# Sorted expert stages of a four-layer gated decoder: silu products kept in PSUM, expert ranks by a scan, row loads led by four jobs, weight splits put behind the normalised rows

## The chip, the cores and the metric

One core of one Trainium2 chip. The metric is the device time of the whole kernel in microseconds, one launch, median over the runs of the same kernel. All data are float32; the large matmuls are done as three fp32r matmuls of a high and a low part of each operand.

## The reference, cut to what matters

x is 8 x 256 rows of 256. Four layers follow one another, each a gated cross attention and a gated feed-forward branch, `x = x + tanh(g) * branch(layernorm(x))`. The change touches the feed-forward branches of layers 1 and 2, both mixtures of 8 experts of which each row takes 2. Layer 2 (layer 1 has hidden size 682, no bias, no shared part, and normalises its two weights):

```python
scores = jax.nn.softmax((xt @ gate_w.T).astype(jnp.float32), axis=-1)
_, idx = jax.lax.top_k(scores + gate_bias, TOPK)
weights = jnp.take_along_axis(scores, idx, axis=1).astype(x.dtype)
y = jnp.zeros_like(xt)
for e in range(N_EXPERTS):
    gate_e = jnp.sum(jnp.where(idx == e, weights, 0.0), axis=1)
    h = jax.nn.silu(xt @ w1[e].T) * (xt @ w3[e].T)
    y = y + gate_e[:, None] * (h @ w2[e].T)
z = jax.nn.silu(xt @ sw1.T) * (xt @ sw3.T) @ sw2.T
return (y + z).reshape(shape)
```

## The kernel before

The kernel is written engine by engine; each engine has one program, in which a function per stage follows the one of the stage before, with semaphores between the engines and an order written out by hand. The two sorted expert stages are the functions `mixture` of each engine, run for `L1F` (layer 1) and `L2F` (layer 2). A stage goes like this.

**Front.** VectorE normalises the 16 tiles of 128 rows (L1230) and writes them to one SBUF tensor. TensorE transposes them (L2175), ScalarE copies them out, TensorE forms the logits (L2165), VectorE the two largest of eight per row by comparing all pairs (L1235 to L1261). TensorE then forms for each row and expert how many rows ahead of it took the same expert (L2183, L2186), and how many there are in all (L2189). VectorE adds the start of the expert's region (L1274), and the result is the row of a DRAM table where GpSimd scatters the normalised row (L772, 32 indirect DMAs). Ahead of the scatter GpSimd splits the first sets of weights (`split_set`, L759 casts to the high part, L761 subtracts for the low part): 2 sets for L1F, 5 for L2F.

**Loop.** A job is 512 rows of one expert; there are 8 fixed jobs, one an expert, and 7 whose expert and rows are read from a table of numbers computed in the front. L2F has four more ahead, the shared experts over all rows, which don't need the table. Per job: SyncE loads the rows (`rows_for`, L515), TensorE transposes them (`turned`, L2205, eight transposes), ScalarE and VectorE make the high and low part (L1318). For each tile of 128 hidden units TensorE runs 12 matmuls of 512 columns (`up`, L1736 to L1738), the half tile of L1F six; ScalarE takes silu of one bank (L1670); VectorE multiplies by the other bank (L1329), casts to the high part (L1332) and subtracts for the low one (L1333). L1F has 5 tiles and a half a job, L2F 2 (4 in a shared job). `down` forms the output of the job in two banks, ScalarE copies them out (L1457), SyncE stores them (L534). The order on TensorE is: tiles 1 to the last of job k, `turned(k + 2)`, tile 0 of job k + 1, `down(k)`. There are two row buffers, two buffers for the transposed rows, and two banks for each of the two products of a tile, so tile n + 2 uses the banks of tile n; TensorE waits for the product of n (`prod`), which frees them:

```python
if n >= 2:
    pe.wait_ge(m["prod"], at["prod"] + n - 1)
```

SyncE's program is a loop over the jobs. Step k: the row load of job k + 2; then, once `down(k)` is done, the weights of set w + ring (L487); then the two stores of the job's result. Only two sets fit in L1F, so a set is asked for when the last but one is used up; in L2F five fit.

**Back.** GpSimd gathers the two results of each row (L786, 32 indirect DMAs), VectorE adds them with their weights to x (L1358).

In what follows the loop of L1F is called A, the routed part of that of L2F is called B. Other lines named: L700 is the inverse square root on GpSimd, L1054 a copy of attention probabilities out of PSUM in other stages. `arena`, `split`, `ew`, `ewh`, `ewl`, `sil`, `lg`, `x` and `w` are SBUF tensors, `bank` is PSUM, `rows_by_expert` the DRAM table.

## Time and profile before

| | us |
|---|---|
| median of 3 runs | 3420.68 (3419.69 to 3465.46) |
| profiled execution, its own time | 3391.78 |
| its span, first to last instruction | 3390.0 |
| TensorE busy, share | 2575.8, 76% |
| VectorE busy, share | 1580.7, 47% |
| ScalarE busy, share | 872.7, 26% |
| GpSimd busy, share | 785.2, 23% |
| mean granted TensorE clock | 0.829 of full |

A granted clock of 1.0 is 2.4 GHz, of 0.5 is 1.2 GHz; a mean between is a mixture of the two. The busy shares are means over many stages, of which the change touches two. In the rows further down a bracket behind an instruction is the idle time of its engine just before it and what ended that; a wait for several semaphores is put down to the one that came last. PE is TensorE's matmuls, PEld its weight loads, DVE VectorE, ACT ScalarE, POOL GpSimd, SPq the DMAs that SyncE issues. fp32 matmuls (not fp32r) are recorded as two.

### The profile page before, as it was taken

The page shows a single profiled execution, that of the slowest core. Times are in us where ns is not written, and L with a number is a line of the kernel's source. Part 1 is how long each engine was busy: PE and PEld are TensorE (multiplying, and loading weights), DVE is VectorE, ACT ScalarE, POOL GpSimd, SP SyncE. Part 2 cuts the span into 40 slices and gives each one's busy share as a digit, 9 for nine tenths or more (in the row PEclk, how much of TensorE's full clock was granted, in tenths as well). Part 3 has the DMA queues.
Part 4 walks back from the last instruction along what each step waited for, and adds up shares of the span by engine and source line. Part 5 has one row for each costly group of instructions (what it writes and reads, how often), then busy time and mean ns, then how long its engine had stood idle before and what let it go on. Part 6 is the DMA issues. An engine that isn't in the chain of part 4 may idle for free.

```text
span 3390.0 us, 37402 instructions
## 1 busy us (share of the span) xinstructions
PE 2575.8 (76%) x13142; PEld 1918.9 (57%) x13142; DVE 1580.7 (47%) x2934; ACT 872.7 (26%) x2012; POOL 785.2 (23%) x709
## 2 busy tenths in 40 slices
PE   3795885487887728888888577673888884999998
PEld 3574554376666625555556466552555653766665
DVE  3443566256657423333334533224564554454454
ACT  1221342111111103323333112122453451232232
POOL 3103223334334133333434422213000000000000
PEclk8795676699898868888989588786896996988899
DMA  3704441122232230000000013321000000000000
GB/s 115 253 0 57 56 60 54 68 96 98 78 103 91 83 118 5 2 2 2 2 2 0 13 50 95 105 86 55 5 3 2 5 1 0 1 0 0 0 0 25
DMA packets 91147, 151.93 MB, mean 45 GB/s; under 512 B 7612, under 2 KB 75900, under 8 KB 88428
## 3 DMA queue, kind: packets, MB, share of 16 engines
q1 hardware_dynamic: 61820, 101.93, 11.1%
q0 software_dynamic: 8736, 27.76, 2.6%
q10 hardware_dynamic: 20496, 20.97, 1.7%
q8 instruction: 59, 0.97, 0.1%
q14 instruction: 36, 0.29, 0.0%
HBM read 90.51 MB, written 47.19 MB: 41 GB/s over the span
## 4 chain that ended last, share of the span: by engine, by line
PE 57%; issue 20%; DVE 10%; POOL 5%; DMA 3%; ACT 3%; SPq 1%; another core or an unknown queue 1%; ACTq 0%; DVEq 0%; POOLq 0%
PE bank L1898 11%; PE bank L1853 7%; PE bank L1736 6%; PE bank L1915 6%; PE bank L1737 5%; PE bank L1738 5%; PE bank L1939 4%; PE bank L1873 2%; DMA arena<-rows_by_expert 2%; POOL arena L786 2%; DVE nmax L1044 1%; PE bank L1987 1%; DVE split L1332 1%; PE bank L2091 1%; ACT arena L1457 1%
## 5 line engine op out<-in xcount | busy, mean ns | idle before, releaser
L1898 PE MATMUL bank<-arena 64*128 64x256 f32 x1536 | 472.4, 442 | 6.2 <-ACT arena L1457 6.2
L1898 PEld LDWEIGHTS bank<-arena 64*128 64x128 f32 x1536 | 283.0, 207 | 141.6 <-issue 108.5
L1542 ACT ACTIVATE arena<-bank,nmax 128x256 f32<-128x256 f32 x512 | 226.3, 470 | 459.8 <-DVE nmax L1044 457.8
L1915 PE MATMUL bank<-ident,arena 128*128 128x128 f32 x1536 | 272.0, 306 | 74.7 <-POOL arena L829 44.2
L1044 DVE TENSOR_REDUCE nmax<-bank 128x2 f32<-128x512 f32 x256 | 175.8, 690 | 321.0 <-PE bank L1898 316.9
L1457 ACT ACTIVATE arena<-bank 128x512 f32<-128x512 f32 (+1 forms) x346 | 198.2, 580 | 463.1 <-PE bank L1853 112.0
L1736 PE MATMUL bank<-split,ewl 128*128 128x512 f32 x514 | 227.3, 442 | 98.8 <-DVE arena L1329 86.2
L1915 PEld LDWEIGHTS bank<-ident,arena 128*128 128x128 f32 x1536 | 177.6, 151 | 210.1 <-issue 112.2
L700 POOL TENSOR_TENSOR rstd<-rstd,mhalf 128x2 f32<-128x2 f32 x40 | 28.0, 700 | 996.8 <-DVE rstd L972 839.2
L1329 DVE TENSOR_TENSOR arena<-sil,bank 128x512 f32<-128x512 f32 x136 | 93.2, 685 | 315.9 <-ACT sil L1670 300.3
L1737 PE MATMUL bank<-split,ewh 128*128 128x512 f32 x514 | 217.2, 423 | 0.0
L1738 PE MATMUL bank<-split,ewh 128*128 128x512 f32 x514 | 215.5, 419 | 0.0
L1333 DVE TENSOR_TENSOR split<-arena,split 128x512 fp32r<-128x512 f32 x136 | 211.9, 1558 | 4.7
L759 POOL CAST ewh<-ew 128x1536 fp32r<-128x1536 f32 (+1 forms) x47 | 91.6, 1948 | 500.0 <-DMA ew<-in_we 500.0
L761 POOL TENSOR_TENSOR ewl<-ew,ewh 128x1536 fp32r<-128x1536 f32 (+1 forms) x47 | 204.2, 4344 | 3.8
L1054 DVE COPY arena<-bank 128x512 f32<-128x512 f32 (+1 forms) x264 | 177.1, 674 | 55.7 <-PE bank L1915 55.6
L1670 ACT ACTIVATE sil<-bank 128x512 f32<-128x512 f32 x136 | 81.4, 598 | 440.5 <-PE bank L1738 413.6
L1736 PEld LDWEIGHTS bank<-split,ewl 128*128 128x128 f32 x514 | 107.9, 210 | 131.5 <-DVE arena L1329 71.5
L1736 PE MATMUL bank<-ewh,split 128*128 128x256 f32 x544 | 167.8, 309 | 17.7 <-DVE split L1333 10.0
L1939 PE MATMUL bank<-arena 128*17 128x256 f32 (+1 forms) x1536 | 157.3, 423 | 24.2 <-ACT arena L1457 16.6
L825 POOL TENSOR_TENSOR esum<-esum,minus 128x2 f32<-128x2 f32 x128 | 89.8, 702 | 326.8 <-ACT arena L1542 326.7
L1737 PE MATMUL bank<-ewl,split 128*128 128x256 f32 x544 | 155.8, 286 | 0.0
(394 smaller groups left out, 4764.7 us busy)
## 6 DMA issues: line engine op xcount, KB each, us to landing
ew<-in_we SPq DMA_DIRECT2D x32, 768.0 KB, 8.0
ew<-in_we SPq DMA_DIRECT2D x15, 1408.0 KB, 6.1
rows_by_expert<-mrow ACTq DMA_DIRECT2D x1, 20480.0 KB, 58.2
arena<-rows_by_expert SPq DMA_DIRECT2D x23, 512.0 KB, 6.5
rows_by_expert<-arena SPq DMA_DIRECT2D x38, 256.0 KB, 5.4
ct<-in_ctxT SPq DMA_DIRECT2D x32, 192.0 KB, 2.4
kpack<-khl SPq DMA_DIRECT2D x48, 128.0 KB, 4.4
qpack<-qhl SPq DMA_DIRECT2D x48, 128.0 KB, 5.8
```

Source lines behind the costliest of these rows:

```text
L761: nc.gpsimd.tensor_tensor(low, whole, high, ALU.subtract).then_inc(m["ws"], 1)
L1044: V.tensor_reduce(nmax[:, h, :], src.rearrange("p (t k) -> p t k", t=T), AXX, ALU.max, negate=True).then_inc(m["mx"], 1)
L1333: tt(lo, whole, hi, ALU.subtract).then_inc(m["hid"], 1)
L1457: return A(dst, src, ACT.Copy)
L1542: ins = A(prob[h % 3][:, t * S:(t + 1) * S], src[:, t * S:(t + 1) * S], ACT.Exp, bias=nmax[:, h, t:t + 1], **kw)
L1736: mm(out_, al, bh, start=start, stop=False)
L1737: mm(out_, ah, bl, start=False, stop=False)
L1738: return mm(out_, ah, bh, start=False, stop=stop)
L1853: ins = mm(dst, w[:, c, gr * P:(gr + 1) * P], of[:, c, :], start=c == 0, stop=c == kt_ - 1 and not s.split)
L1898: ins = mm(bank[h % 3][:, t * S:(t + 1) * S], q[r0:r0 + 64, gr, t * P:(t + 1) * P], kT[r0:r0 + 64, gr, :], start=True, stop=True)
L1915: ins = tr(bank[3 + k % 2][:, c0:c0 + P], prob[k % 3][:, t * S + kt * P:t * S + (kt + 1) * P], ident[:, :])
L1939: ins = mm(bank[5 + gr // 2 % 2][r0:r0 + s.vs, gr % 2 * S:(gr % 2 + 1) * S], v[:, kt, h * s.vs:(h + 1) * s.vs], probT[h % 8][:, kt * S:(kt ...
```

## The change

Five edits.

1. The product silu x second projection is written back over the PSUM bank it reads, instead of to SBUF. The cast and the subtraction that make its high and low part read it there. The bank is therefore released at the end of the subtraction (`hid`) and not of the product (`prod`).
2. The ranks: one matmul with ones gives for each tile of rows and expert the number of rows in that tile, one with the strict triangle the number ahead within the tile. VectorE sums over the tiles by a scan along a row, restarted at each expert by a constant 0/1 tensor `within`, subtracts the tile's own count, and adds the number within the tile.
3. SyncE's step k loads the rows of job k + 4 instead of k + 2; four loads stand ahead of the loop of L1F and two, as before, ahead of that of L2F. The number of row buffers stays two, so the load of k + 4 still waits until job k + 2 is transposed.
4. GpSimd waits for all 16 normalised tiles before it starts to split weights.
5. Two memsets more among the constants at the start, for `within`.

```diff
-            r.hid = [(split[:, k * 1024:k * 1024 + 512], split[:, k * 1024 + 512:k * 1024 + 1024],
-                      arena[:, k * 1024 + 512:k * 1024 + 1024]) for k in range(s.slots)]
+            r.hid = [(split[:, k * 1024:k * 1024 + 512], split[:, k * 1024 + 512:k * 1024 + 1024])
+                     for k in range(s.slots)]
...
-                if not s.shared:
-                    rows_for(0)
-                    rows_for(1)
+                for k in range(s.first, s.first + 2 if s.shared else 4):
+                    rows_for(k)
                 for k, job in enumerate(s.jobs):
                     e = k - s.first
-                    if s.first <= k + 2 < len(s.jobs):
-                        rows_for(k + 2)
+                    if max(s.first + 2, 4) <= k + 4 < len(s.jobs):
+                        rows_for(k + 4)
...
+            nc.gpsimd.memset(within[:, :, :], 1.0).then_inc(g["consts"], 1)
+            pool.wait_ge(g["consts"], done[0] + 1)
+            nc.gpsimd.memset(within[:, :, 0:1], 0.0).then_inc(g["consts"], 1)
...
                 root({"asked": asked[s.name]}, 1, rstda[:, :], rstda[:, :], mhalf[:, 0:NT])
+                pool.wait_ge(g["xn"], entered(s.name, B) * T)
                 for w in range(s.ring):
                     split_set(w)
...
-                ch.link(tt(part[2], bank[1][:, 0:NT * NE].rearrange("p (t e) -> p t e", e=NE),
-                           ebase[:, 0:1, :].broadcast_to(full), ALU.add))
+                ch.link(V.tensor_tensor_scan(upto[:, :, :].rearrange("p e t -> p (e t)"), within[:, :, :].rearrange("p e t -> p (e t)"),
+                                             bank[1][:, 0:NT * NE], 0.0, ALU.mult, ALU.add))
+                before = scr[:, 384:384 + NT * NE].rearrange("p (e t) -> p e t", e=NE)
+                ch.link(tt(before, upto[:, :, :], bank[1][:, 0:NT * NE].rearrange("p (e t) -> p e t", e=NE), ALU.subtract))
+                ch.link(tt(before, before, bank[1][:, NT * NE:2 * NT * NE].rearrange("p (e t) -> p e t", e=NE), ALU.add))
+                ch.link(tt(part[2], before.rearrange("p e t -> p t e"), ebase[:, 0:1, :].broadcast_to(full), ALU.add))
...
-                rows_of = bank[1][:, NT * NE:NT * NE + NE]
+                rows_of = upto[:, :, NT - 1]
...
-                    hi, lo, whole = (t[rr, :] for t in r.hid[n % s.slots])
+                    hi, lo = (t[rr, :] for t in r.hid[n % s.slots])
+                    whole = bank[(2 if rr.start == 0 else 0) + n % 2][rr, :]
...
-                    tt(whole, sil[n % 2][rr, :], bank[(2 if rr.start == 0 else 0) + n % 2][rr, :], ALU.mult)\
-                        .then_inc(m["prod"], 1)
+                    tt(whole, sil[n % 2][rr, :], whole, ALU.mult).then_inc(m["prod"], 1)
...
-                mm(bank[1][:, 0:NT * NE], strict[:, :], lg[:, :, :].rearrange("p t e -> p (t e)"), start=True, stop=False)
-                for t in range(NT - 1):
-                    n = NT - 1 - t
-                    mm(bank[1][:, (t + 1) * NE:NT * NE].rearrange("p (k e) -> p k e", e=NE), ones[:, :],
-                       lg[:, t:t + 1, :].broadcast_to([P, n, NE]), start=False, stop=t == NT - 2)
-                for t in range(NT):
-                    ins = mm(bank[1][:, NT * NE:NT * NE + NE], ones[:, :], lg[:, t, :], start=t == 0, stop=t == NT - 1)
+                chosen = lg[:, :, :].rearrange("p t e -> p e t")
+                for k, w in ((0, ones), (1, strict)):
+                    ins = mm(bank[1][:, k * NT * NE:(k + 1) * NT * NE].rearrange("p (e t) -> p e t", e=NE), w[:, :], chosen,
+                             start=True, stop=True)
...
                     if n >= 2:
-                        pe.wait_ge(m["prod"], at["prod"] + n - 1)
+                        pe.wait_ge(m["hid"], at["hid"] + n - 1)
```

In SyncE's queue, at the start of the loops' row loads of L2F (the first load below is that of jobs 4 and 5, `ew` a weight set, `rows_by_expert<-arena` the stores of a job), before:

```order
L515 DMA arena<-rows_by_expert 128x4x256 x2
L487 DMA ew<-in_we 128x1536 x2
L515 DMA arena<-rows_by_expert 128x4x256
L487 DMA ew<-in_we 128x1536
L534 DMA rows_by_expert<-arena 128x2x256 x2
L515 DMA arena<-rows_by_expert 128x4x256
```

and now:

```order
L516 DMA arena<-rows_by_expert 128x4x256 x4
L488 DMA ew<-in_we 128x1536 x2
L516 DMA arena<-rows_by_expert 128x4x256
L488 DMA ew<-in_we 128x1536
L534 DMA rows_by_expert<-arena 128x2x256 x2
L516 DMA arena<-rows_by_expert 128x4x256
```

The pattern behind is the same, but four row loads instead of two stand ahead of the first weight load, so that each load between two jobs' stores is that of a job two further on.

On TensorE, the ranks of L1F (`lg` holds the chosen experts; L2205 and L2211 are the first transposes of the loop), before:

```order
L2183 MATMUL bank<-lg,strict 128x128
L2186 MATMUL bank<-lg,ones 128x120
L2186 MATMUL bank<-lg,ones 128x112
L2186 MATMUL bank<-lg,ones 128x104
...
L2186 MATMUL bank<-lg,ones 128x8
L2189 MATMUL bank<-lg,ones 128x8 x16
L2205 MATMUL bank<-ident,arena 128x128 x8
```

and now:

```order
L2194 MATMUL bank<-lg,ones 128x128
L2194 MATMUL bank<-lg,strict 128x128
L2211 MATMUL bank<-ident,arena 128x128 x8
```

32 matmuls have become two. On VectorE, behind them (`upto` is the scan's result, `scr` scratch), before:

```order
L1274 TENSOR_TENSOR scr<-bank,ebase 128x128
L1277 TENSOR_TENSOR scr<-scr,larger 128x128
```

and now:

```order
L1279 SCALAR_TENSOR_TENSOR upto<-within,bank 128x128
L1282 TENSOR_TENSOR scr<-upto,bank 128x128
L1283 TENSOR_TENSOR scr<-scr,bank 128x128
L1284 TENSOR_TENSOR scr<-scr,ebase 128x128
L1286 TENSOR_TENSOR scr<-scr,larger 128x128
```

Three steps more stand between the matmuls and the slots.

## Rows read from the trace of the kernel before

**Rows 1.** Stretches of the span: busy us per engine, granted clock, DMA share, GB/s.
```profile
...
646.00:1181.00 535.00, 435.90 (x2190) 359.24 (x2190) 325.63 (x300) 89.35 (x151) 185.43 (x55) 0.90 0.26 87
...
2047.00:2285.00 238.00, 164.25 (x812) 140.69 (x810) 71.06 (x115) 49.27 (x85) 59.08 (x24) 0.81 0.33 101
...
```

**Rows 2.** Single lines: duration ns min/median/max, first and last start us, forms.
```profile
L1329 DVE TENSOR_TENSOR arena<-sil,bank x136: 673/687/692, 661.6 to 2278.2; 128x512 f32<-128x512 f32 x121, 64x512 f32<-64x512 f32 x15
L1332 DVE CAST split<-arena x136: 424/426/2798, 662.3 to 2278.9; 128x512 fp32r<-128x512 f32 x121, 64x512 fp32r<-64x512 f32 x15
L1333 DVE TENSOR_TENSOR split<-arena,split x136: 689/693/6541, 662.8 to 2279.4; 128x512 fp32r<-128x512 f32 x121, 64x512 fp32r<-64x512 f32 x15
L1054 DVE COPY arena<-bank x264: 324/681/693, 1279.5 to 3372.2; 128x512 f32<-128x512 f32 x128, 128x160 f32<-128x160 f32 x4
L1670 ACT ACTIVATE sil<-bank x136: 589/599/617, 660.9 to 2277.5; 128x512 f32<-128x512 f32 x121, 64x512 f32<-64x512 f32 x15
```

**Rows 3.** Timeline of one job of A, GpSimd and VectorE: start us, us, instruction.
```profile
1051.39 2.54 POOL L759 CAST ewh<-ew 128x2816 fp32r<-128x2816 f32 x1 [21.57 <-DMA ew<-in_we]
1054.01 6.20 POOL L761 TENSOR_TENSOR ewl<-ew,ewh 128x2816 fp32r<-128x2816 f32 x1
...
1054.25 6.51 DVE L1333 TENSOR_TENSOR split<-arena,split 128x512 fp32r<-128x512 f32 x1
```

**Rows 4.** Timeline of the same job, TensorE; in brackets idle time before and releaser.
```profile
1047.16 0.39 PE L1736 MATMUL bank<-split,ewl 128*128 128x512 f32 x1
...
1049.88 0.39 PE L1736 MATMUL bank<-split,ewl 128*128 128x512 f32 x1
...
1061.41 0.80 PE L1736 MATMUL bank<-split,ewl 128*128 128x512 f32 x1 [5.93 <-DVE arena L1329]
...
1066.97 0.47 PE L1736 MATMUL bank<-split,ewl 128*128 128x512 f32 x1 [0.93 <-DVE arena L1329]
...
1070.02 0.35 PE L1736 MATMUL bank<-ewh,split 128*128 128x256 f32 x1
```

**Rows 5.** Timeline of A, ScalarE: second result half of jobs 0, 10 and 13.
```profile
686.79 0.60 ACT L1457 ACTIVATE w<-bank 128x512 f32<-128x512 f32 x1 [4.47 <-PE bank L1738]
...
1044.37 0.60 ACT L1457 ACTIVATE w<-bank 128x512 f32<-128x512 f32 x1 [4.47 <-PE bank L1738]
...
1152.85 0.60 ACT L1457 ACTIVATE w<-bank 128x512 f32<-128x512 f32 x1 [4.47 <-PE bank L1738]
```

**Rows 6.** Waits in B (us in total, times, longest), then timeline of one job.
```profile
PE bank L2205 <- DMA arena<-rows_by_expert: 70.5, 13, 6.8
...
2099.46 0.56 SPq L515 DMA_DIRECT2D arena<-rows_by_expert  x1
...
2106.29 1.97 PE L2205 MATMUL bank<-ident,arena 128*128 128x128 f32 x8 [5.50 <-DMA arena<-rows_by_expert]
...
2112.14 0.28 PE L1736 MATMUL bank<-ewh,split 128*128 128x256 f32 x1
...
2115.02 0.40 PE L1736 MATMUL bank<-split,ewl 128*128 128x512 f32 x1
```

**Rows 7.** Waits ahead of loop A, 540 to 590.
```profile
PE bank L2175 <- DVE arena L1230: 22.5, 5, 7.7
```

**Rows 8.** Timeline ahead of loop A, and the router's first step ahead of B.
```profile
543.26 30.12 DVE L1230 TENSOR_SCALAR arena<-x,mva,rstda 128x256 f32<-128x256 f32 x16 [3.08 <-POOL rstda L700]
...
579.61 0.29 DVE L1235 COPY lg<-bank 128x128 f32<-128x128 f32 x1 [6.23 <-PE bank L2165]
...
587.86 0.79 PE L2183 MATMUL bank<-lg,strict 128*128 128x128 f32 x2 [8.29 <-DVE idle L1260]
...
601.79 0.29 DVE L1274 TENSOR_TENSOR scr<-bank,ebase 128x128 f32<-128x128 f32 x1 [12.20 <-PE bank L2189]
...
1911.37 0.29 DVE L1235 COPY lg<-bank 128x128 f32<-128x128 f32 x1 [9.84 <-PE bank L2165]
```

**Rows 9.** Waits in the shared jobs, 1940 to 2000.
```profile
ACT sil L1670 <- remote: 26.9, 2, 14.2
```

More of the change, by code:

```diff
@@ L32 @@
 NBLK = NT * P // 512
-N_CONSTS = 69
 DYN = 7
@@ L370, in build @@
         second = sb("second", [P, NT, NE])
+        upto = sb("upto", [P, NE, NT])
+        within = sb("within", [P, NE, NT])
         gw = sb("gw", [P, 2, NT])
@@ L660, in _ @@
             select(strict[:, :], 0.0, 0, [[1, P]], -1, ALU.is_gt)
+            pool.wait_ge(g["consts"], done[0])
+            nc.gpsimd.memset(within[:, :, :], 1.0).then_inc(g["consts"], 1)
+            pool.wait_ge(g["consts"], done[0] + 1)
+            nc.gpsimd.memset(within[:, :, 0:1], 0.0).then_inc(g["consts"], 1)
+            done[0] += 2
             for e in range(NE):
@@ L665, in _ @@
             g["n_consts"] = done[0]
-            assert done[0] == N_CONSTS, done[0]
             pool.dma_start(w01, a["w01"]).then_inc(g["w0f_in"], 16)
@@ L2236, in down @@
                                 ins = mm3(bank[4 + i][:, j * D:(j + 1) * D],
-                                          [t[rr, q * P:(q + 1) * P] for t in r.hid[(s.a0[k] + n) % s.slots][0:2]],
+                                          [t[rr, q * P:(q + 1) * P] for t in r.hid[(s.a0[k] + n) % s.slots]],
                                           [cut_[3][rr, h, :] for cut_ in expert(s, w)], n == 0, n == len(s.tiles[k]) - 1)
```

## Prediction

> **What bounds the kernel now.** I read first the table of stretches, then the waits inside the two sorted expert stages, then the timeline of one job of each, last the stretch ahead of each loop. The stretch 646 to 1181 is the expert loop of layer 1 (A), 2047 to 2285 the routed part of that of layer 2 (B): together 773 of the 3390 us. TensorE is busy 81% and 69% of them, at a granted clock of 0.90 and 0.81 [rows 1]. The reader is to see that TensorE is the engine to keep busy in both, and that something else stops it in each.
>
> In A it is VectorE, held by GpSimd. The step that stores the low half (L1333) reads two SBUF tensors; it takes 0.69 us as a rule and up to 6.54; the copy ahead of it (L1332) 0.43, and up to 2.80. The product (L1329), which reads one operand from PSUM, never took over 0.692, and copies out of PSUM (L1054) never over 0.693 [rows 2]. In one job the long one starts at 1054.25 and ends at 1060.76, half a microsecond behind the GpSimd subtraction of the weight split, 1054.01 + 6.20; it could only start when that was done [rows 3]. Behind them the product of the next tile is late, and TensorE waits for it: 5.93 us, then 0.93, and after the 5.93 its matmuls restart at the 1.2 GHz level, 0.43 us each instead of 0.23 [rows 4]. A job lasts 35.85 us: second result half of job 0 at 686.79, of job 13 at 1152.85, 13 periods [rows 5].
>
> In B it is the load of the rows: 13 waits, 70.5 us. The load is issued at 2099.46, behind the stores of the job before, and lands when TensorE has stood 5.50 us; then eight transposes take 1.97 us, about twice what they cost at the high level, and some seven matmuls run at the low level [rows 6].
>
> **The change, part by part.** The sum is made against the profiled execution, 3391.78 us (span 3390.0), 28.9 below the median of the runs, 3420.68; I carry the difference over unchanged.
>
> *Products in PSUM.* The copy now reads PSUM: 0.68 by L1054 instead of 0.43; the low half reads PSUM and SBUF, 0.69 by L1329. Neither form was ever held [rows 2], so I take both as free of GpSimd. No row has VectorE writing PSUM; bounds 0.43 (the median copy) and 2.8 us (the longest copy, held), I take 0.69, that of the same operation writing SBUF. A tile then costs VectorE 3 x 0.69 + 0.09 = 2.16 us, below the tile pitch of TensorE, 2.72 [rows 4].
> The price: a bank is free only at the end of all three steps, and tile n + 2 waits for that. A tile's twelve matmuls take 2.72, the last one's tail 0.2, silu 0.6 and a hand-over of 0.1, then 2.2: 5.8, against 2 x 2.72 = 5.44 until the bank is wanted. So 0.4 us late at every other full tile, about 1.2 a job of A, 0.4 in each of the 4 shared jobs ahead of B, none in a routed job, where the down projection lies between.
> What is late next in A is the weights. The set for the next job is asked for when the last down projection ends (1044.37), GpSimd starts on it at 1051.39, 7.0 later [rows 3, 5]. Cast and subtraction 8.8, then the first tile of that job and the down projection of this one, 1066.97 to 1080.1 and the result half, 13.2 [rows 4]. Period 7.0 + 8.8 + 0.1 + 13.2 = 29.1. TensorE alone would need 26.1 (4.5 tiles and the next job's first at 2.72, transposes 0.9, down 10.1, the last two read off rows 4) and 1.2, so 27.3; it idles 1.8 us, and the extra bank wait is hidden in 13 periods and paid in jobs 0 and 14. I take no fall of the clock: behind 0.93 us of idle it stayed at the high level [rows 4]; were it to fall, 13 x 2.4 = 31 us come back. Gain: 13 x (35.85 - 29.1) = 88, less 2.4: 85.
>
> *Loads lead by four jobs.* There are still two row buffers, so the load of job k + 4 waits until job k + 2 is transposed. SyncE issues it in step k, ahead of that step's weight load and stores; both wait for the down projection of k, which TensorE runs after that transposition, so nothing queued behind it is later. The load then has two jobs, some 18 us, against its 5 to 7. A routed job of B becomes 0.9 + 2 x 2.72 + 2.88 = 9.2 us [rows 4, 6]. The stretch of 238 us holds 15 jobs and 1 us of result copies: 237 now, 138 after. Gain 99, of which 70.5 is the wait and the rest the low clock behind it. Traffic per job is 0.75 + 0.5 + 0.5 MB in 9.2 us, 195 GB/s, over twice the 101 measured in the stretch now [rows 1]; that is the weak place of this term. The shared jobs pay 4 x 0.4. Net 97. In A the row load was hidden already: nothing.
>
> *Ranks by a scan.* Now 32 matmuls between 587.86 and 601.79, 13.9 us with nothing beside them; after, two of the first kind. The first took 0.79 with its end, so 1.5 for two. VectorE gets three more steps of 128 elements: the one step of this shape (L1274) takes 0.29, with its gap 0.33; the scan has no row, bounds 0.29 and 0.69 (the product of 512), I take 0.4. Net 13.9 - 1.5 - 1.1 = 11.3, in each of the two stages [rows 8]: 22.6. GpSimd starts the scatter as soon as the slots are there, its splits being done, so this is on the path.
>
> *Splits wait for the normalised rows.* The 16 normalisations take 30.12 us because each waits for a GpSimd instruction [rows 8]; an unheld copy of twice the elements takes 0.43 [rows 2], so 6.9 is the bound for all, and I take 5. TensorE waited 22.5 us for them, 7.7 of that before the first [rows 7]. It would reach its last logits 16 us earlier. But the splits now start 3 to 5 us later (by rows 3, 8.8 us for 2816 columns: 27 us for the two sets of A, 25 for the five of 1536 columns of B) and run beside the router steps, of which eight or more read two SBUF tensors, as L1333 does. Each that meets a split waits for its end. Laid out step by step, the first such step 16 us ahead of where the router begins now (579.61 in A, 1911.37 in B), one of them let through at each end of a split instruction, and the rest free behind the last split, the masks come 6 us earlier in A and 9 in B.
> The Trainium skill, "SBUF — State Buffer", section "Who interferes with whom", says that a two-input VectorE step with both inputs in SBUF contends with a GpSimd instruction that reads SBUF, and that a reduction never does. The long rows of L1333 agree. By it the hold stands; without it the two gains would be 16 each.
> The page "VectorE: DVE Perf Modes", in its section on the TRN2 errata, prices a PSUM source 62 cycles above an SBUF one; my estimate from that is 0.06 us more for each of the steps on PSUM. The rows show none of it, 0.687 beside 0.693, and the measurement decides.
>
> Sum: 85 + 97 + 22.6 + 15 = 220. Profiled execution 3172, timed 3200. What I take as unchanged: the 26.9 us that ScalarE stands in the shared jobs, while the scatter runs, for a releaser outside the engines [rows 9].
>
> **Rivals.**
> 1. *The weight chain of A is longer*: the load lands a microsecond later, and the clock falls in each gap. 13 x 1 + 31, less what overlaps: about 38 us more, 3238. For it: the stores of the job before are queued right behind the load and share its engines; against it: they do so now.
> 2. *The router steps are not held*, or the ScalarE stall is shorter by one of its two pieces: 17 or 14 us less, 3184. Against it: rows 2.
> 3. *The copy or the low half is still held with its operand in PSUM.* Then A keeps its stalls, and TensorE waits for the end of the low half instead of the product, some 5 us more a job: +70 instead of -85 in A. 3200 + 155 = 3355, within 2%. Against it: 136 products and the copies of L1054, none held.
> 4. *The loads still come late in B*, because the queue is full at 195 GB/s: the 97 are lost, 3297.
> 5. *Slower.* VectorE's steps that write or read PSUM are dear: at s us each, a tile is 3s + 0.09, and above 2.72 VectorE sets the pace of all 136 tiles. Its other work in the loops is about 51 us (two low parts of 0.65 in each of 34 jobs, sums into x in four). The loops have now 535 and 238 us [rows 1], less 9 ahead of the first tile, and 70 for the shared jobs (4 x 17.6: four tiles, transposes, a down projection twice that of a routed job): 834. The fronts give 37. Break-even is 136 (3s + 0.09) + 51 = 871, s = 1.98 us; over 2% slower from s = 2.15. At 2.3: 3550. For it only that no row writes PSUM.
>
> **How the numbers follow.** Chances: forecast 0.62, rival 1 0.12, 2 0.09, 3 0.05, 4 0.09, 5 0.03. About 2% is what a measurement of this kernel can tell from no change. Faster by over 2% (below 3352): all but rivals 3 and 5, 0.93, to be cut a little for a mix of 3 and 4, 0.92. Within 2%: 0.05. Slower: 0.03. The range holds the forecast, rivals 1 and 2, and half of 4: from 3165 to 3265.
>
> **What would show it.** Right: no copy or low-half step over 0.75 us; waits of TensorE for the product gone, in A a wait of 1 to 2 us a job for the split instead; period of A 29.1, routed job of B 9.2 with a clock near 1.0; two rank matmuls; the normalisations within 5 us, yet router steps of 2 to 6 us beside the splits. Wrong: a VectorE step writing PSUM at over 0.9 us; a row load that ends a wait in B; a period of A over 31; the ScalarE stall of another size.

## The result, and the profile after

The changed kernel took 3194.99 us in the median of four runs, against 3439.75 us of the kernel before in the same session (four runs). Of its runs, 3164.04, 3165.89, 3224.09 and 9230.50 us, the comparison uses the first two: the third had a lower mean clock (0.830 against 0.85), and nothing on record explains the fourth. The ratio is 0.9197, with a 95% interval from 0.9061 to 0.9333. In a second session it was 3210.42 us in the median of six runs, ratio 0.9397, 0.9319 to 0.9475. So the change makes the kernel faster by 6 to 8%, far over the 2% that a measurement tells from no change.

Forecast were 3200 us for the runs and 3172 for the profiled execution; measured were, in the first session, 3164 and 3166 for the runs, of which the first is the profiled one. The two lie on the lower end of the range that I gave, 3165: their middle, 3164.97, is 0.03 us below it and 35 us below the forecast.

| stage, us of the profiled executions | before | after | gain | forecast |
|---|---|---|---|---|
| start to the normalised rows of layer 1 | 543.3 | 544.1 | -0.8 | 0 |
| normalised rows to first scatter, layer 1 | 61.1 | 43.6 | 17.5 | 17.3 |
| first scatter to first gather, layer 1 | 585.5 | 494.5 | 91.0 | 85 |
| from there to the normalised rows of layer 2 | 684.8 | 684.0 | 0.8 | 0 |
| normalised rows to first scatter, layer 2 | 63.1 | 42.3 | 20.8 | 20.3 |
| first scatter to first gather, layer 2 | 349.9 | 254.6 | 95.3 | 97 |
| from there to the end | 1102.3 | 1099.0 | 3.3 | 0 |

The boundaries are starts of instructions in the timeline: the first normalisation, the first indirect DMA of a scatter, the first of a gather. I call the two "scatter to gather" stages the loop stages of A and of B; that of B holds the four shared jobs too. The forecast column is the prediction's four terms laid on these stages (11.3 + 6, 85, 11.3 + 9, 97).

Stretches of the kernel after, as in [rows 1]: A, and the routed part B.

```profile
629.00:1074.00 445.00, 411.55 (x2190) 337.40 (x2190) 206.58 (x300) 89.26 (x151) 180.10 (x56) 0.98 0.32 105
1912.00:2062.00 150.00, 144.70 (x868) 128.30 (x866) 81.71 (x124) 50.04 (x87) 59.73 (x24) 0.98 0.50 157
```

TensorE is now busy 92% and 96% of the two, where it was 81% and 69%, and the granted clock is 0.98 in both. VectorE's busy time in A fell from 325.6 to 206.6 us for the same 300 instructions: that is the held time, less the 0.27 us that each copy now costs more.

The lines of [rows 2], after. The product (now L1339) writes its own bank, the copy (L1341) and the low half (L1342) read it.

```profile
L1339 DVE TENSOR_TENSOR bank<-sil,bank x136: 682/696/706, 643.4 to 2052.2; 128x512 f32<-128x512 f32 x121, 64x512 f32<-64x512 f32 x15
L1341 DVE CAST split<-bank x136: 690/691/696, 644.2 to 2053.0; 128x512 fp32r<-128x512 f32 x121, 64x512 fp32r<-64x512 f32 x15
L1342 DVE TENSOR_TENSOR split<-bank,split x136: 690/691/695, 644.9 to 2053.7; 128x512 fp32r<-128x512 f32 x121, 64x512 fp32r<-64x512 f32 x15
L1279 DVE TENSOR_TENSOR_SCAN upto<-within,bank x2: 419/420/420, 584.0 to 1804.8; 128x128 f32<-128x128 f32 x2
```

Look at the maxima: 706, 696 and 695 ns where 6541 and 2798 stood. The longest of all 408 steps is 0.01 us above its median.

Waits of TensorE in A, then in B (us in total, times, longest), as in [rows 6] for B.

```profile
PE bank L1745 <- POOL ewl L765: 15.5, 13, 2.5
PE bank L1745 <- DVE split L1342: 6.6, 29, 0.7
PE bank L1745 <- issue: 3.3, 1, 3.3
```

```profile
PE bank L1745 <- issue: 3.2, 2, 3.0
```

In A what is late next is the weight split, 13 times, as forecast, and the bank at 0.23 us a time. In B no row load ends a wait, where there were 13 of them, 70.5 us.

One period of A in the timeline, from one weight load to the next (SyncE's DMA, ScalarE's second result half, GpSimd, TensorE), then the result halves of jobs 0 and 13, as in [rows 5].

```profile
698.53 0.83 SPq L488 DMA_DIRECT2D ew<-in_we  x2
...
704.82 2.54 POOL L763 CAST ewh<-ew 128x2816 fp32r<-128x2816 f32 x1 [14.36 <-DMA ew<-in_we]
...
707.43 6.25 POOL L765 TENSOR_TENSOR ewl<-ew,ewh 128x2816 fp32r<-128x2816 f32 x1
...
713.74 0.50 PE L1745 MATMUL bank<-split,ewl 128*128 128x512 f32 x1 [0.81 <-POOL ewl L765]
...
726.72 0.83 SPq L488 DMA_DIRECT2D ew<-in_we  x2
```

```profile
670.48 0.60 ACT L1466 ACTIVATE w<-bank 128x512 f32<-128x512 f32 x1 [4.47 <-PE bank L1747]
...
1042.85 0.60 ACT L1466 ACTIVATE w<-bank 128x512 f32<-128x512 f32 x1 [4.47 <-PE bank L1747]
```

The load takes 6.3 us until GpSimd starts, cast and subtraction 8.9, tile and down projection 13.0: 28.2 in this job. Over the 13 jobs the time from the result half to GpSimd's start is 6.1 to 7.2 us, 6.6 in the mean, and the whole period is (1042.85 - 670.48) / 13 = 28.64, against 35.85 before and 29.1 forecast.

Two routed jobs of B by their transposes, 9.27 us apart (forecast 9.2), at the high level of the clock.

```profile
1968.37 1.04 PE L2211 MATMUL bank<-ident,arena 128*128 128x128 f32 x8
...
1977.64 1.04 PE L2211 MATMUL bank<-ident,arena 128*128 128x128 f32 x8
```

Ahead of A, the rows that answer to [rows 8]: normalisations, the router's first steps, the two rank matmuls, and GpSimd's first scatter of layer 2.

```profile
544.07 5.26 DVE L1235 TENSOR_SCALAR arena<-x,mva,rstda 128x256 f32<-128x256 f32 x16 [3.08 <-POOL rstda L704]
565.00 0.29 DVE L1240 COPY lg<-bank 128x128 f32<-128x128 f32 x1 [15.67 <-PE bank L2174]
...
565.64 6.24 DVE L1242 TENSOR_TENSOR sel<-lg,gm 128x128 f32<-128x128 f32 x1
571.92 2.36 DVE L1256 TENSOR_TENSOR scr<-lg 128x1024 f32<-128x1024 f32 x1
...
575.57 3.07 DVE L1258 TENSOR_TENSOR scr<-lg 128x1024 f32<-128x1024 f32 x1
...
582.19 0.81 PE L2194 MATMUL bank<-lg,ones 128*128 128x128 f32 x2 [17.23 <-DVE idle L1265]
582.82 0.65 PE L2194 MATMUL bank<-lg,strict 128*128 128x128 f32 x2
...
1808.53 1.12 POOL L777 DMA_INDIRECT rows_by_expert<-arena,sli  x1 [12.22 <-DVE idle L1292]
```

The normalisations take 5.26 us instead of 30.12, and the router starts at 565.00 instead of 579.61; but its first step with two SBUF inputs stands 6.24 us beside a split where it would take 0.29, and two of the steps of 1024 elements stand 2.36 and 3.07 instead of 1.22. The masks come 5.67 us earlier in the span (582.19 against 587.86). The stage itself began 0.81 us later than before (544.07 against 543.26), so 6.5 us of some 15.4 reach the masks, where I had said 6. In layer 2 the held steps are others, of 2.32, 1.43 and 4.40 us.

### The profile page after: what moved, and what is told of

It is laid out like the page before. It is cut to its first block, busy times and chain, and to the rows that moved or that the text cites. A ratio compares the mean times of both kernels' runs of the same rounds, so it can differ in the third digit from the quotient of the medians.

```text
span 3162.2 us, 37172 instructions
## 1 busy us (share of the span) xinstructions
PE 2500.6 (79%) x13022; PEld 1853.0 (59%) x13022; DVE 1441.3 (46%) x2940; ACT 871.5 (28%) x2012; POOL 779.9 (25%) x711
## 4 chain that ended last, share of the span: by engine, by line
PE 57%; issue 18%; POOL 8%; DVE 8%; DMA 4%; ACT 3%; another core or an unknown queue 1%; SPq 1%; DVEq 0%; ACTq 0%; POOLq 0%
PE bank L1907 12%; PE bank L1862 8%; PE bank L1924 6%; PE bank L1745 5%; PE bank L1948 5%; PE bank L1747 4%; PE bank L1746 4%; PE bank L1882 3%; POOL ewl L765 3%; DMA ew<-in_we 3%; POOL arena L791 2%; DVE nmax L1049 2%; PE bank L1996 1%; PE bank L2100 1%; PE bank L2129 1%
## 5 line engine op out<-in xcount | busy, mean ns | idle before, releaser
L1745 PE MATMUL bank<-split,ewl 128*128 128x512 f32 x514 | 213.0, 414 | 36.5 <-DVE split L1342 20.7
L1339 DVE TENSOR_TENSOR bank<-sil,bank 128x512 f32<-128x512 f32 x136 | 94.8, 697 | 307.0 <-ACT sil L1679 287.9
L1746 PE MATMUL bank<-split,ewh 128*128 128x512 f32 x514 | 203.9, 397 | 0.0
L1747 PE MATMUL bank<-split,ewh 128*128 128x512 f32 x514 | 203.5, 396 | 0.0
L1745 PE MATMUL bank<-ewh,split 128*128 128x256 f32 x544 | 168.6, 310 | 12.8 <-issue 6.6
L1948 PE MATMUL bank<-arena 128*17 128x256 f32 (+1 forms) x1536 | 158.7, 428 | 22.9 <-ACT arena L1466 15.2
L1747 PE MATMUL bank<-ewh,split 128*128 128x256 f32 x544 | 156.7, 288 | 0.0
L1745 PEld LDWEIGHTS bank<-split,ewl 128*128 128x128 f32 x514 | 98.1, 191 | 76.1 <-DVE split L1342 24.4
```

The costliest lines, as they stand in the source:

```text
L1745: mm(out_, al, bh, start=start, stop=False)
L1746: mm(out_, ah, bl, start=False, stop=False)
L1747: return mm(out_, ah, bh, start=False, stop=stop)
L1948: ins = mm(bank[5 + gr // 2 % 2][r0:r0 + s.vs, gr % 2 * S:(gr % 2 + 1) * S], v[:, kt, h * s.vs:(h + 1) * s.vs], probT[h % 8][:, kt * S:(kt ...
```

## The experiments

All ten kernels were timed with the kernel before on the same chip. Four have one part of the change each, on the kernel before; they, like all others, are read by stage as in the table above. The kernel before itself was profiled in the first session alone, so where its stages are compared with those of these kernels, two sessions are compared.

**Part one alone: the products in PSUM.**

```diff
-                    hi, lo, whole = (t[rr, :] for t in r.hid[n % s.slots])
+                    hi, lo = (t[rr, :] for t in r.hid[n % s.slots])
+                    whole = bank[(2 if rr.start == 0 else 0) + n % 2][rr, :]
...
-                        pe.wait_ge(m["prod"], at["prod"] + n - 1)
+                        pe.wait_ge(m["hid"], at["hid"] + n - 1)
```

> The kernel before with the first edit alone: products in PSUM, the bank released at the end of the low half. Theory 1 (VectorE was held by GpSimd through its SBUF operands, next is the weight chain): jobs 0 to 13 of A take 13 x 28.6 instead of 13 x 35.85 us, 94 less; B as before; no copy or low-half step over 0.75 us; profiled execution 3392 - 94 = 3298. Theory 2 (part of the 94 came from the earlier row loads, which no longer share the DMA engines with the weights in A): 31 to 33 us a job, 3330 or more. On the offset between profiled execution and timed runs: if it is fixed, the timed median is 29 above the profile; if it is a state of the clock, it differs from kernel to kernel and follows the granted clock listed with each run.

Measured: 3301.75 us, ratio 0.9733 (0.9658 to 0.9808). The loop stage of A is 491.0 us, its job (1065.83 - 696.09) / 13 = 28.44; the loop stage of B is 320.8, as in the other kernels of that session that keep the old row loads (319.4 and 323.5). Waits of TensorE in A:

```profile
PE bank L1736 <- POOL ewl L761: 14.6, 13, 2.2
PE bank L1736 <- DVE split L1333: 6.6, 30, 0.7
```

This edit alone has the whole gain of A, 94.5 us against the first session's 585.5, and 94 to 98 against the three kernels of its own session that keep the old products (584.9, 588.3, 589.0); and it has the same two waits as the changed kernel. By time alone neither this edit nor the next is clear of the 2%: both intervals end at 0.981.

**Part two alone: row loads lead by four.**

```diff
-                    if s.first <= k + 2 < len(s.jobs):
-                        rows_for(k + 2)
+                    if max(s.first + 2, 4) <= k + 4 < len(s.jobs):
+                        rows_for(k + 4)
```

> The kernel before with the loads led by four jobs alone. Theory 1: no wait of TensorE for rows in B, the 15 jobs there 9 to 10 us each, 85 to 90 us less than before, A unchanged within 3 us; profiled execution about 3303. Theory 2 (in B too VectorE would now be held by the weight splits, since product and low half still stand in SBUF, and the freed time brings the two together): part of the gain is lost, jobs of 11 to 14 us, 3330 to 3360.

Measured: 3290.59 us, ratio 0.9725 (0.9643 to 0.9807). The loop stage of B is 225.5 us, against 319.4 and 323.5 in the two kernels without the edit on the same chip: 96 us. That of A is 589.0, no gain. No row load ends a wait of TensorE in B, and the stretch shows 149 GB/s at a DMA share of 0.48. That is the traffic that I had called the weak place of the term, though as the mean of a stretch it stays below the 195 that I had worked out for a job:

```profile
1966.00:2116.00 150.00, 148.18 (x896) 131.41 (x896) 107.60 (x138) 43.87 (x76) 66.63 (x36) 1.00 0.48 149
```

**Part three alone: ranks by a scan.**

```diff
-                for t in range(NT - 1):
-                    n = NT - 1 - t
-                    mm(bank[1][:, (t + 1) * NE:NT * NE].rearrange("p (k e) -> p k e", e=NE), ones[:, :],
...
+                for k, w in ((0, ones), (1, strict)):
+                    ins = mm(bank[1][:, k * NT * NE:(k + 1) * NT * NE].rearrange("p (e t) -> p e t", e=NE), w[:, :], chosen,
+                             start=True, stop=True)
```

> The kernel before with the ranks by two matmuls and a scan alone. Theory 1: 11.3 us less in each of the two stages, profiled execution 3392 - 23 = 3369. Theory 2 (GpSimd's splits are what the scatter waits for): less than 15 us in all. In before GpSimd was idle 32 and 38 us ahead of the scatter, which speaks for theory 1.

Measured: 3382.98 us, ratio 0.9976 (0.9876 to 1.0076): by time alone it can't be told from nothing. By stage it can. Normalised rows to scatter take 51.9 us in layer 1, where the kernels with the old ranks and the old splits took 62.9 and 63.0 in these sessions, and 51.8 in layer 2 against 63.1: 11.0 and 11.3 us. The scan takes 0.42 us, the two matmuls 1.28 from the first one's start to the second one's end.

**Part four alone: splits behind the normalised rows.**

```diff
+                pool.wait_ge(g["xn"], entered(s.name, B) * T)
                 for w in range(s.ring):
                     split_set(w)
```

> The kernel before with the splits put behind the normalised rows alone. Theory 1 (normalisation unheld, router steps held instead): 6 us less in the stage of layer 1, 9 in that of layer 2, profiled execution 3377. Theory 2 (the hold is only moved and gives nothing): within 3 us of 3392.

Measured: 3362.17 us, ratio 0.9893 (0.9785 to 1.0002). The two stages are 54.6 and 53.7 us: 8.3 and 9.4 us of gain. With part three, 62.9 - 11.0 - 8.3 = 43.6 and 63.1 - 11.3 - 9.4 = 42.4, and the changed kernel has 43.6 and 42.3. The four ratios multiplied give 0.934, beside 0.9397 measured in the second session: within these errors the parts don't help or hinder each other, and the stages say the same.

**The changed kernel again**, in the second session.

> The changed kernel once more, without any edit. Theory one, the four edits save a fixed time in four stages and everything else follows the granted clock: loop A 494 to 496 us, loop B 225 to 226 us without the ScalarE stall in the shared jobs or 254 to 255 us with it, the stages ahead of the scatters 43.6 and 42.3 us, and a run's time falls with its mean granted clock; the ratio to the kernel before is 0.93 to 0.935 (220 to 240 us of some 3400). Rival, part of the gain of the first comparison belongs to the chip and session and not to the change: the ratio comes out above 0.945 while the stages stay as they were.

Measured: 3210.42 us, 0.9397 (0.9319 to 0.9475): between the two expectations, with both in its interval. The stages decide for the first theory; those ahead of the last are as in the first session within 2 us (542.1, 43.6, 493.4, 685.1, 42.3, 253.2). The first stage varies by 10 us over all kernels (540.7 to 551.0) and the last by far more, though nothing in either is changed. The stretch from the first gather of layer 2 to the end, by kernel: one with the new wait on the old products (below), before, changed, part one alone, part two alone, and the changed kernel in this second session (3243.83 us, mean clock 0.825). Columns as in [rows 1].

```profile
2295.70:3383.20 1087.50, 879.41 (x4704) 615.79 (x4704) 558.51 (x1164) 364.77 (x812) 48.71 (x51) 0.87 0.03 7
```

```profile
2287.70:3390.00 1102.30, 895.52 (x4704) 625.29 (x4704) 560.34 (x1164) 365.00 (x812) 48.64 (x51) 0.85 0.02 7
```

```profile
2063.20:3162.20 1099.00, 893.62 (x4704) 623.81 (x4704) 559.08 (x1164) 364.41 (x812) 48.59 (x51) 0.85 0.02 7
```

```profile
2172.60:3300.50 1127.90, 925.05 (x4704) 641.80 (x4704) 561.88 (x1164) 364.92 (x812) 48.53 (x51) 0.83 0.02 7
```

```profile
2168.30:3316.40 1148.10, 950.15 (x4704) 653.33 (x4704) 559.82 (x1164) 365.28 (x812) 48.39 (x51) 0.80 0.02 7
```

```profile
2059.90:3241.90 1182.00, 987.34 (x4704) 673.79 (x4704) 562.71 (x1164) 365.87 (x812) 48.71 (x51) 0.78 0.02 7
```

The same 4704 matmuls, TensorE busy 879 to 987 us, VectorE, ScalarE and GpSimd alike to 1%; what differs is the granted clock, 0.87 down to 0.78, and the stretch is 95 us longer with it. The changed kernel has both one of the shortest and the longest of them. The other profiled executions lie between (1111.7 to 1138.6). The runs' times go the same way: the kernel before took 3360.66 us at a mean clock of 0.832 and 3410.17 at 0.814 on one chip, the changed one 3174.29 at 0.846 and 3211.91 at 0.835 in its second session.

**The new wait without the new place.** The wait that the change adds, on the kernel before, with the products still in SBUF. This is the price that my third rival named.

```diff
-                        pe.wait_ge(m["prod"], at["prod"] + n - 1)
+                        pe.wait_ge(m["hid"], at["hid"] + n - 1)
```

> The kernel before with one line changed: TensorE takes the next bank only when the low half of the product two tiles back is written, not when the product is. The product still goes to SBUF, so this is the wait that the change adds, without what the change saves. Theory one, the three VectorE steps of a tile with two SBUF inputs are what loop A pays (they lie 4.1 us behind ScalarE's result and a bank is then late by some 5 us a job): a job of A takes about 41 us in place of 35.9, loop A is some 65 to 70 us longer than the kernel before, and the whole 2% slower. Rival, the saving of the change lies in the earlier steps, and the wait costs nothing since the low half is always done in time: loop A stays at 585 us.

Measured: 3429.95 us, ratio 1.0064 (1.0012 to 1.0117); the loop stage of A is 596.4 us, 11 more than before and not 65 (and 11 more than the 584.9 of the next kernel, which was timed in the same session), a job (1164.17 - 685.78) / 13 = 36.80. Waits of TensorE in A here, then in the kernel before:

```profile
PE bank L1736 <- DVE split L1333: 97.9, 26, 7.8
```

```profile
PE bank L1736 <- DVE arena L1329: 86.2, 25, 6.0
```

The releaser has changed, the sum by 12 us. My price of 5 us a job was wrong, both for rival 3 and here: I had added a held step to each wait. In the kernel before, the product that TensorE waited for (start 1060.68) stood already behind the held low half of the tile before it, which ended at 1060.76 with the split on GpSimd. Here TensorE waits for that low half itself, stops one tile earlier, and goes on at the same end of a hold:

```profile
1025.53 6.48 DVE L1333 TENSOR_TENSOR split<-arena,split 128x512 fp32r<-128x512 f32 x1
...
1032.06 0.79 PE L1736 MATMUL bank<-split,ewl 128*128 128x512 f32 x1 [7.48 <-DVE split L1333]
```

So the saving of part one is the end of the holds. The later release costs 11 us in the loop with the holds, and with the products in PSUM TensorE waits 6.6 us in all for the bank.

**The change less part one.** Products back in SBUF and the bank released by the product again, the other three parts kept.

```diff
-                    whole = bank[(2 if rr.start == 0 else 0) + n % 2][rr, :]
+                    hi, lo, whole = (t[rr, :] for t in r.hid[n % s.slots])
```

> The changed kernel with the products back in SBUF and the bank released by the product, the other three parts as changed. Theory one, the parts are independent: loop A goes back from 494 to 585 us, loop B stays at 254 us (its jobs are not held by these steps once the rows come early) or 226 us without the ScalarE stall, and the time is some 90 us above the changed kernel. Rival, the earlier row loads of layer 1 or the later splits carry a part of loop A's gain: loop A comes out under 575 us, or loop B above 260 us.

Measured: 3280.81 us, ratio 0.9589 (0.939 to 0.9788). Loop of A 584.9, loop of B 254.4, both as theory one says; the parts are independent in this direction too. In B the old VectorE steps cost nothing, though they are held there as well: the copy takes 1.41 us in the mean of 29 copies of the routed jobs instead of its bare 0.43.

**A finer weight split in A**, on the changed kernel: three cuts, and TensorE's first tile waits for its own columns alone.

```diff
-                    for part in range(s.parts):
-                        q, n = s.loaded(w, part)
+                    for cut in range(s.cuts):
+                        q, n = s.loaded(w, 1 if cut == 2 else 0)
...
+                    if h == 0 or s.cuts == 3 and h in (1, s.ft - 1):
+                        pe.wait_ge(m["ws"], at["ws"] + w * s.cuts + (3 if h == s.ft - 1 and h > 0 else h + 1))
```

> The changed kernel with layer 1's weight split in three cuts (the first tile's columns, the other whole tiles, the half tile with the down projection), so that TensorE's first tile of a job waits for the first cut alone. Theory one, a job of loop A is bound by the chain weight load, split on GpSimd (6.25 us for a half) and TensorE's first tiles, with the load and the last split as fixed ends: the waits of TensorE on the split (15.5 us in 13) go, a job takes 27.3 us in place of 28.64, and loop A is 17 us shorter. Rival, TensorE's own work and the VectorE holds bound the job already: loop A moves by under 4 us.

Measured: 3204.92 us, ratio 0.9436 (0.9357 to 0.9514), a profiled loop stage of A of 483.9 us, 9.5 below the changed kernel in the same session; a job (1029.0 - 669.77) / 13 = 27.63. Waits of TensorE in A:

```profile
PE bank L1756 <- DVE split L1353: 11.2, 40, 1.1
PE bank L1756 <- POOL ewl L776: 0.8, 3, 0.3
```

The mechanism holds: the waits for the split fall from 15.5 to 0.8 us. But not all of it is gained, since the waits for the bank rise from 6.6 to 11.2: TensorE, no longer stopped once a job, meets them more often. A job gains 1.0 us instead of 1.34; of the 13 us that this gives over 13 jobs the stage keeps 9.5, since the jobs at its two ends came out longer. The timed ratio doesn't show it, with an error of this size.

**Fewer splits ahead of the scatter**, on the changed kernel.

```diff
-                for w in range(s.ring):
+                for w in range(3 if s.shared else 1):
...
-                for w in range(s.ring, s.sets):
+                for w in range(3 if s.shared else 1, s.sets):
```

> The changed kernel with only one weight set (A) or three (B) split on GpSimd ahead of the scatter and the others behind it, so that fewer router steps on VectorE are held by a split. Theory one, what is left of the holds after the wait lies in the router's steps (6.24, 2.36 and 3.07 us of A, 2.3, 1.4 and 4.4 us of B): the stage from the normalised rows to the scatter falls from 43.6 to about 35 us in A and from 42.3 to about 36 us in B. Rival, the scatter itself and the blocks' table set the end of that stage: it moves by under 2 us, and what it does give comes back as a first job that waits for its weights.

Measured: 3168.31 us, ratio 0.9293 (0.9216 to 0.937). The stages from the normalised rows to the scatter are 34.7 and 36.0 us, 8.9 and 6.3 less, and the loops are not longer for it (492.2 and 252.1). The router's first two-input step, 6.24 us in the changed kernel's layer 1, is free in both layers:

```profile
L1242 DVE TENSOR_TENSOR sel<-lg,gm x2: 291/292/292, 568.7 to 1780.0; 128x128 f32<-128x128 f32 x2
```

**Both**, on the changed kernel.

> Both edits of the two kernels beside it on the changed kernel. Theory one: the two gains add, 17 us in loop A and some 14 us ahead of the scatters, about 31 us below the changed kernel in the same session (ratio to the kernel before some 0.92 where the changed kernel has 0.93). Rival: with splits behind the scatter, the first jobs of A wait for their weights, and the sum is under 20 us.

Measured: 3167.90 us in the median of six, ratio 0.9309 (0.9239 to 0.9379), 42.5 us below the median of the changed kernel in the session, or (0.9397 - 0.9309) x 3400 = 30 us by the ratios. The stages that the edits touch give the cleaner figure: 34.7, 481.9, 36.0 and 254.0 against 43.6, 493.4, 42.3 and 253.2, that is 8.9 + 11.5 + 6.3 - 0.8 = 26 us of the 31 expected. The intervals of the two ratios overlap, so that this version beats the changed kernel is shown by the stages, not by the times; that it beats the kernel before is shown by both.

## Why the prediction was right, and where it failed

- **Products in PSUM**, forecast 85 us, measured 91.0 together and 94.5 alone. The mechanism is shown: no step was held, the bank wait is 0.23 us a time, the next late thing is the weight split. The size was off in the period, 28.64 instead of 29.1, and 13 x 0.46 = 6 us is the difference. The term that was too dear is "7.0 later" for the weight load, read off one late job: over the 13 jobs it is 6.6 us in the mean, and it was 6.7 in the kernel before.
- **Bank wait "0.4 us late at every other full tile"**: 0.23 in 29 waits, 6.6 us, where 1.2 a job would be 18 in 15 jobs. A part of it lay inside the wait for the weights, as forecast: with that wait gone it is 11.2 us. The rest was forecast too dear.
- **Loads lead by four**, forecast 97, measured 95.3 together and 96 alone. The job of 9.2 is 9.27. The 195 GB/s were called "over twice the 101"; they are 1.9 times, and the stretch shows 157.
- **Ranks**, forecast 11.3 each, measured 11.0 and 11.3. The scan at 0.42 was taken at 0.4. In layer 1 the scan starts 1.77 us after the first matmul and not 1.5, and not because of the matmuls: VectorE is at other steps of the router until then.
- **Splits wait**, forecast 6 and 9, measured 8.3 and 9.4 against stages of 62.9 and 63.1 us. In the first session the stage of layer 1 before was 61.1, shorter than in the three other kernels that share it (62.9 to 63.0), and there the gain is 6.5; why it was shorter stays open. Here the rule of the Trainium skill, "SBUF — State Buffer", section "Who interferes with whom", decided: by it the two gains are some 15 us, without it 32. The runs agree with it twice. The held steps are there (6.24, 2.36, 3.07), and when the splits are taken away the steps fall to their bare 0.29 and 1.22 and the stages by 15.2 us. The copy out of PSUM and the reductions between them (0.29 and 1.22) were free throughout.
- **The dearer PSUM source of the Trainium skill, "VectorE: DVE Perf Modes", section on the TRN2 errata**, 62 cycles or, by my estimate, 0.06 us a step: not seen in the steps with two inputs. The product is 0.696 with PSUM on both sides against 0.687, the low half 0.691 with a PSUM input against 0.693 without. For the copy the price is 0.27 us (0.691 against 0.426), which I had from L1054.
- **The step that failed** is the first sentence of the working, "28.9 below the median of the runs, 3420.68; I carry the difference over unchanged". The four terms, 220, came out as 224.6 in the first session's profile, the span fell by 227.8, and the profiled execution was forecast at 3172 and took 3164. But the 28.9 us are no fixed cost around the program. They are how far that one execution lay from the median, and the experiments show what it is made of: the last stage alone runs from 1087 to 1182 us as the granted clock goes from 0.87 to 0.78, and the changed kernel stands at either end of that range (1099 and 1182). The profiled execution of before was one of the quick ones there (1102), and by their times the other runs then were not; the changed kernel's first two runs were quick again (mean clock 0.849 and 0.850). For the changed kernel the offset between the profiled execution and the middle of those two was 0.9 us and not 28.9. So of the 35 us by which the 3200 lay too high, 28 are the offset and 8 the sum. In the second session it had the other sign: the profiled execution, 3243.83, lay 33 us above the median. That the 3200 lie near the medians, 3194.99 and 3210.42, is luck: the first of them is the middle between 3165.89 and 3224.09 only because a run of 9230 us counts among the four, and the centre was a guess on the clock of another run. The 0.03 us that lie between the two runs and the range mean nothing by themselves; the 35 us to the centre do. What failed with it is the range: its lower end, 3165, was made from rivals of the change alone, with nothing in it for the clock, though the before runs already spread over 46 us.
- **The rivals.** 1 (a longer weight chain) fell: the load is shorter, the clock 0.98. 2 had two halves. Router steps were held in the kernels that have the later splits (in part four alone again 6.24, 2.36 and 3.07 us), until fewer splits stood there. The stall of ScalarE in the shared jobs was not shorter in the first session, 26.2 us in two waits where there were 26.9; but the four kernels with one part each, all timed on one chip, had none, and a loop stage of B some 28 us shorter, while all those profiled on two other chips had it, 26.2 to 32.0 us, the kernel before with the new wait alone among them. In the first session it falls to both kernels alike, so it doesn't touch the gain. What it is stays open; the trace names only a releaser outside the engines. 3 and 5 (held or dear steps) fell with the first line of the profile, and the price of 3 was wrong too, 0.95 us a job instead of 5. 4 (loads still late) fell: 157 GB/s went through with no wait for rows.

What stays open: whether the change itself lowers the clock in the last stage a little. The medians of the second session differ by 215 us and the stages ahead of the last by 224 to 230, so some 10 to 15 us may be given back there. The last stage is 1132 us in the mean of the six profiled executions that have the new loads, ranks and splits together, and 1119 in that of the six others, which points the same way; but single ones spread over 95 us, so it is not shown.

## What to carry to other kernels

Where VectorE shares its time with GpSimd, keep the intermediate of a chain in PSUM rather than in SBUF: here three steps at 0.69 us beat steps of 0.43 and 0.69 that now and then stood 6.5, and the longer hold on the bank cost TensorE 0.23 us at every third tile. Price a later release by where the hold ends and not by adding steps up: here it cost 0.95 us a job and not 5. A row load that came 5 us late in each job needed only to be issued two jobs earlier, with no buffer more. Forecast by stage, and give the time of the runs a range of its own from the granted clock in the long unchanged stages: on this kernel that is 60 to 95 us, many times the errors of the four terms together (8 us).

## What was unexpected of the hardware

- A step of VectorE that reads and writes the same PSUM bank costs what one writing SBUF does: 0.696 against 0.687 us for 512 fp32 columns.
- The scan over 128 elements, one input from PSUM, takes 0.42 us where a plain two-input step of the size takes 0.29.
- An unchanged stage of 4704 matmuls took between 1087.5 and 1182.0 us from one execution to another, with the granted clock at 0.87 to 0.78, and the mean clock of a run tells its time: 50 us for 0.018 (3360.66 at 0.832, 3410.17 at 0.814).
- To wait for the end of three VectorE steps instead of the first cost 0.95 us a job of five and a half tiles, though the three together could stand over 8 us.
